# A four-layer graph network on one core: output scatters and table gathers of the last stage issued in turn

## The reference, cut to what matters

```
h = relu(layernorm(x));  x = x + spmm(spmm(h))              # two weighted sums over the edges
h = relu(layernorm(x));  x = x + norm-weighted segment_sum((h @ W)[src]) + b
h = relu(layernorm(x));  x = x + mlp(h + segment_sum(h[src]))
h = relu(layernorm(x));  x = x + mlp([h, segment_sum(mlp([h[src], h[dst], edge_attr]))])
```

## Time and profile before

| | us |
|---|---|
| median of 3 runs | 4624.67 (4622.48 to 4624.89) |
| span of the profiled execution | 5754.7 |
| last stage in the trace | about 4080 to 5754.7 |
| one step of the last stage in the trace, steady part | 122.9 |

### The profile page before, as it was taken

One profiled execution on the slowest core, in us unless ns is written; L12 is line 12 of the kernel. 1 busy time (PEld: TensorE's weight loads), 2 busy tenths in 40 slices (PEclk: granted clock), 3 DMA queues, 4 the chain that ended last, 5 costly groups with the idle time before them and its releaser, 6 DMA issues. The chain is left out here.

```text
span 5754.7 us, 60611 instructions
## 1 busy us (share of the span) xinstructions
PE 3759.0 (65%) x18706; PEld 3006.2 (52%) x18706; DVE 3033.3 (53%) x7288; ACT 2016.3 (35%) x5132; POOL 3313.7 (58%) x2843
## 2 busy tenths in 40 slices
PE   3776666676999975565556777763566655666665
PEld 2544444446898964444445555553454444455454
DVE  4644444455556546665665766755454434455442
ACT  2444444451111113443444444431233333333332
POOL 4888888887888874444332554553444554445544
PEclk7776666675555557887888777875778877777787
DMA  8333333334444432222222333333121111121110
GB/s 293 51 51 51 51 51 51 51 42 73 87 81 87 87 40 82 78 93 79 96 77 75 108 125 123 112 107 130 54 91 55 59 57 57 54 91 55 60 54 21
DMA packets 335488, 452.10 MB, mean 79 GB/s; under 512 B 208111, under 2 KB 233301, under 8 KB 334740
## 3 DMA queue, kind: packets, MB, share of 16 engines
q1 hardware_dynamic: 159268, 361.69, 17.8%
q0 software_dynamic: 176000, 87.72, 12.5%
HBM read 258.41 MB, written 225.53 MB: 84 GB/s over the span
## 5 line engine op out<-in xcount | busy, mean ns | idle before, releaser
L929 POOL DMA_INDIRECT ga<-table,isl x784 | 783.9, 1000 | 278.1 <-issue 231.3
L1059 POOL DMA_INDIRECT out_x<-acc,osl x392 | 430.0, 1097 | 755.6 <-DVEq L80 640.4
L997 POOL DMA_INDIRECT xu<-acc,osl x392 | 625.1, 1595 | 144.6 <-issue 103.1
L1205 PE MATMUL tp<-xw,cc 128*128 128x394 f32 x784 | 411.5, 623 | 345.8 <-DVE cc L2011 215.4
L1242 PE MATMUL tp<-us,wide 128*128 128x64 f32 x1568 | 416.8, 422 | 87.4 <-DVE us L2139 49.2
L929 POOL DMA_INDIRECT ga<-xu,isl x392 | 394.0, 1005 | 121.5 <-issue 116.5
L1205 PEld LDWEIGHTS tp<-xw,cc 128*128 128x128 f32 x784 | 141.5, 220 | 603.1 <-issue 325.4
L1093 PE MATMUL mm<-ident,wide 128*128 128x128 f32 x1176 | 213.1, 343 | 355.6 <-DVE wide L2218 275.7
L1242 PEld LDWEIGHTS tp<-us,wide 128*128 128x128 f32 x1568 | 380.0, 332 | 92.2 <-DVE us L2139 49.4
L1255 PE MATMUL tp<-acc,wide 128*128 128x64 f32 x1560 | 423.3, 427 | 0.8
L1093 PEld LDWEIGHTS mm<-ident,wide 128*128 128x128 f32 x1176 | 180.0, 182 | 406.1 <-issue 323.2
(11 more groups left out here) (378 smaller groups left out, 9513.8 us busy)
## 6 DMA issues: line engine op xcount, KB each, us to landing
wide<-xu SPq DMA_DIRECT2D x84, 448.0 KB
zx<-key_rows SPq DMA_DIRECT2D x28, 896.0 KB
out_x<-wide SPq DMA_DIRECT2D x56, 448.0 KB, 3.4
table<-acc SPq DMA_DIRECT2D x56, 448.0 KB, 2.5
xf<-xs SPq DMA_DIRECT2D x56, 448.0 KB
wide<-table SPq DMA_DIRECT2D x56, 448.0 KB
xu<-in_x SPq DMA_DIRECT2D x25, 1000.0 KB
hop_even<-zeros SPq DMA_DIRECT2D x1, 12544.0 KB
```

The lines of the kernel that those rows point to most:

```text
L929: nc.gpsimd.indirect_dma_start(o[:, g, :], None, table, bass.IndirectOffsetOnAxis(idx[:, g:g + 1], 0)).then_inc(s, 16)
L997: nc.gpsimd.indirect_dma_start(xu, bass.IndirectOffsetOnAxis(osl[b][:, g:g + 1], 0), acc[b][:, g, :], None, compute_op=ALU.add).then_inc(f ...
L1059: nc.gpsimd.indirect_dma_start(out, bass.IndirectOffsetOnAxis(osl[b][:, g:g + 1], 0), acc[b][:, g, :], None, bounds_check=nodes_max, oob_i ...
L1205: f.key_row.raise_by(nc.tensor.matmul(tp[1][:, at:at + KEYS], reach[:, g * P:g * P + P], key_steps, start=True, stop=True), ("g", b, g))
```

## The change

POOL's order in steps 2 to 11 of the last stage. A new function takes the place of one call each of `t_scatter` and `t_gather`: for each b it waits for everything that both need, and then issues one scatter and one gather in turn for each of the 14 columns. Nothing is added or removed, and the counts on all semaphores stay as they are.

```
+            def t_both(i, n):
+                for b in B2K:
+                    after.wait_ge(*tt.o_ready.at(i, ("o", b)))
+                    after.wait_ge(tt.written[b], 16 * G * i)
+                    after.wait_ge(*tt.ga_free.at(n - 1, ("g", b)))
+                    for g in range(G):
+                        nc.gpsimd.indirect_dma_start(
+                            out, bass.IndirectOffsetOnAxis(osl[b][:, g:g + 1], 0), acc[b][:, g, :], None,
+                            bounds_check=nodes_max, oob_is_err=False).then_inc(tt.written[b], 16)
+                        gather(ga[b], tables[1], isl[b], tt.got_a[b], (g,))
+
             for i in range(2, STEPS - 2):
-                t_scatter(i - 1)
-                t_gather(i + 2)
+                t_both(i - 1, i + 2)
```

## The result

The changed kernel takes 5060.68 us (median of 4 runs, 5059.87 to 5061.3) against 4624.78 for the one before (4 runs, 4622.48 to 4625.35): a ratio of 1.0942, 95% interval 1.0926 to 1.0957. That is 435.9 us more, 43.6 for each of the ten changed steps. Predicted were 5044 and 41.9.

The account below looks back on a forecast made before the run. Timed, POOL (74.8 us a step) and the compute chain (75.1) were taken as about even. New step 95.3 + 21.7 = 117.0, 41.9 more; ten steps add 419 to 4624.7, giving 5044 us, range 4895 to 5105.

Parts of the forecast that it names:

- ACT stands at b = 1 until 95.3: ACT, before writing `acc[1]`, waits for the last scatter to land at 95.3 us of the pass, 43.3 later than before.
- late start: POOL's first scatter waits for `ga_free`, so its burst runs from 20.8 to 95.3 us of the pass, not 0 to 74.5.
- tail: From ACT's row for b = 1 to the next `o_ready`: 23.1 us in the profile before, 21.7 forecast after the change.
- the gathers' circle: Last gather landed, DVE's second add, `isl` copies, next burst: 77.6 us a step if ACT's wait does not decide.
- the bounds: If the compute chain is faster than 75.1 us a step, POOL's 74.8 takes its place and the result hardly moves.
- the range: Cold matmuls after ACT's long stand could give 2 or 3 us a step back; left out of the central forecast.
- the hole: DVE's 40.93 and 8.73 us waits for PE's products in a last-stage step, until POOL's burst ends; claimed only while recorded.
- A: Rival: the hole is in timed runs too and shifts with POOL's burst, +20.7 a step, +207, 4832 us; chance 0.09.
- B: Rival: ACT's wait does not decide, only the gathers' circle is left, +2.5 a step, +25, 4650 us; chance 0.03.
- C: Rival: POOL's burst sets the step, its stretched scatters disappear in turn with gathers, 2.6 us less a step, 4599; chance 0.02.
- The signs named in advance: In the changed profile: POOL's wait ends 20.7 us later, DMAs alternate at 1.28 and 1.25, recorded step grows by about 20.7.
- the 1.4 kept for them: POOL's turns between scatter and gather: at most 28 x 0.05 = 1.4 us a step, left for the range.

Follow-up runs that it names:

- three landings: Kernels differing only in burst order, last scatter of b = 1 at 28th, 42nd or 55th (the change) of 56: steps 88.0, 102.3, 119.4 us.
- the first experiment: The kernel before, profiled once more with no edit: 4626.81 us, with a span of 4625.0.
- the last set: Runs of the longer kind, with the changed kernel again, nothing new edited: 5962.65 us against 5832.39 for the kernel before, ratio 1.0216.

## Why the prediction was right

**The direction and the mechanism.** "ACT stands at b = 1 until 95.3" is what happened. Since the burst itself starts 20.8 us into the pass, that is 74.5 behind its start, and ACT's row lies 74.8 behind it. The table of three landings shows it, and so do the 394 us that come back when ACT need not wait. Taking away either term does not leave the other's share: 394 come back without ACT's wait, 181 without the late start, 428 without both. While ACT waits, the two terms stand one behind the other (late start, burst, tail), so both count in full; once it does not, the late start costs only the few us of the gathers' circle.

**The sum.** The loss is 43.6 us a step, and 41.9 were forecast. Two terms were off, partly against each other. The step before is 76.1 and not 75.1, because POOL sets it. The 75.1 was worked out for the compute chain, which needs only 71.7; that it lies near POOL's number is luck, though the bounds had said that POOL's 74.8 would take its place. The step without gathers, less its whole wait, would have given the chain: 83.8 - 12.0 = 71.8. The new step is 119.6 and not 117.0: the way from ACT's row to the next burst is 44.6, where 21.7 + 20.8 = 42.5 were forecast. Nearly all of these 2.1 us is the clock of TensorE, which the prediction had left for the range with 2 or 3 us. This is what the changed kernel's PE does behind ACT's wait:

```profile
4148.98 5.20 PE L1110 MATMUL mm<-vt,u 128*128 128x512 f32 x8 [24.06 <-ACT vt L1506]
...
4158.94 3.23 PE L1110 MATMUL mm<-vt,u 128*128 128x512 f32 x8
```

The same work at the same place of the trace from which the tail of 23.1 was read, with a granted clock of 1.00:

```profile
4917.14 3.27 PE L1100 MATMUL mm<-vt,u 128*128 128x512 f32 x8 [0.23 <-ACT vt L1496]
```

The windows of the changed kernel (columns as above), for the stretch of the first row, for the one after it, and for the whole step:

```profile
4148.98:4155.50 6.52, 6.52 (x22) 3.85 (x23) 0.00 (x0) 4.72 (x11) 0.00 (x0) 0.70 0.00 0
4155.50:4160.00 4.50, 4.50 (x35) 4.01 (x34) 1.56 (x5) 2.18 (x3) 0.00 (x0) 1.00 0.00 0
4071.55:4190.99 119.44, 70.06 (x441) 55.51 (x439) 57.13 (x120) 42.17 (x79) 58.14 (x56) 0.79 0.21 64
```

The same for a step of the kernel before, of the first experiment:

```profile
4009.61:4090.83 81.22, 68.28 (x440) 55.32 (x439) 57.11 (x121) 42.21 (x78) 62.92 (x60) 0.92 0.31 96
```

After 24 us of standing PE gets a granted clock of 0.70 on the average of the first 6.5 us, so part of them at the lower of its two levels (1.2 GHz), and the eight matmuls take 5.20 us. At 1.00 eight take 3.23, and 3.27 in the trace of before: 1.9 us of the 2.1. The two whole steps show the same busy times on PE, DVE and ACT within 3%, and 38 us of difference in length (the step of before shown is the longest of its ten). So next to nothing got slower; the engines wait for each other in turn.

**The reason for the hole.** Here the prediction was wrong. "I conclude that the hole exists only while the execution is recorded": the first experiment was recorded without it, in 4625.0 us, and the changed kernel too, in 5059.5 where 5962 was forecast. In the last set the hole was in runs of a median of 5962.65, and the recorded one of them timed 5963.41 with a span of 5961.1. So the hole belongs to some executions, recorded or not, and what decides which is open: two sets ran on the same chip, one with and one without it, and within each set all runs were of one kind. Nor is the difference only in the last stage: its first waiting gather begins at 4058.67 in the long recording of before and at 3521.42 in the short one, so some 540 of the 1130 us lie ahead of it. What had carried the conclusion was the comparison of the span with the timed runs, 5754.7 against 4624.67, and that held: the profile was of another kind of execution than the median. Only the cause put to it was false. The forecast needed no more than that the timed runs lack the hole; for executions with it, it would have been wrong, 419 us where 130 were measured. The Trainium skill ("Runtime: NRT & Kernel Launch", section on the preamble and postamble) gives a nearly fixed gap of 6.2 us between a profile's total and the reported time, the total being the longer. A small and nearly fixed gap is what the runs show, but between span and time, and with the time the longer: 1.8 us (4626.81 and 4625.0), 1.8 (5061.3 and 5059.5), 2.3 (5963.41 and 5961.1). It should have made me look for two kinds of executions, not for a cost of recording. No run shows the mechanism of "NOTIFIC — the notification-queue block" (section 7.1) at work.

**The rivals.** A holds in direction where the hole is (+130, not +207), and not in the runs that were to be forecast. B's circle exists but decides only where ACT's wait is gone (81.0 a step; it was worked out as 77.6, with a burst 3 us too short). C named the right bound and a real effect, POOL's stretched instructions, but they do not vanish: the changed kernel's burst is 74.9, since an instruction of POOL in that order is stretched beside DVE too, a gather as well as a scatter (4121.12: 1.64 us, as DVE has its two operations of line 2430 from 4120.89). The signs named in advance came out so: scatters and gathers alternate at 1.32 and 1.27 us, not 1.28 and 1.25, and the turns cost 0.5 to 1 us a step, within the 1.4 kept for them; ACT is seen to wait for the scatters; and the recorded step is 119.4, not 143.6, since the hole is not in that recording.

## What to carry to other kernels

When two sequences on one queue are interleaved, the waits of both move to the front of the first, and the completion of the first moves to the end of the second: ask who waits for that completion, and compute the step as that landing plus the chain behind it. Compare the span with the timed runs before adding anything up: where they differ by far, the profile is of another kind of execution, and its waits need not be in the timed one, whatever their cause. If the order is wanted, double the buffer that the late completion holds: a second `acc` gave back 394 of the 436 us here. And a total that does not move can hide two changes: by the traces the kernel before, given a second `acc`, lost 8.1 us in the steady steps and won 7.4 in the last pass.

## What the hardware showed that I had not expected

- POOL's indirect DMAs are stretched from 0.98 to between 1.65 and 1.70 us beside DVE's operations on two f32 operands of 128x896 from SBUF in lines 2440, 2444 and 2448 (2.09 us for two operations), and are normal at once behind them. With DVE's second operand in PSUM they stay at 0.98. The Trainium skill ("SBUF — State Buffer", on DMAs issued from the GpSimd queue) tells of descriptors held up by DVE's 2-port modes, with an f32 copy as the example. These rows show a milder stretch, by 0.7 us for each, beside operations that take about 1.0 us for 896 elements each.
- The landing of a scatter is not a fixed 2.2 us: with the 16 DMA engines full of SP's plain transfers (share 1.04) it was 5.5. That the one causes the other was not tested by itself.
- One kernel has two durations, 4625 and 5745 to 5832 us, and a change has two prices: 1.094 in one kind of execution and 1.022 in the other. In the longer kind PE, ACT and DVE stand or creep while POOL issues indirect DMAs. The granted clock over the whole is 0.72 against 0.78 for the kernel before, and 0.71 against 0.755 for the changed one. What brings it about was not tested.
